# Moving 42 of the weight-scale sums from the attention into the projection, and evicting a finished tile earlier in the DVE's order

## The reference

```
x = x + attn(layernorm(x));  x = x + ffn(layernorm(x))
attn: q, k, v = x@W + x@A@B (16 query heads, 4 key/value heads of 128, rank 16)
      rms norm and rotation of q and k, causal softmax attention -> y
      y minus its part along v;  out = y@Wproj + y@p_A@p_B
ffn:  every weight matrix W (8192 x 2048) becomes clip(round(W/s), -1, 1) * s, s = mean(|W|) + 1e-8
      down(silu(up(x)) * gate(x))
```

## Time and profile before

| | |
|---|---|
| median of three executions | 3892.86 us (3891.25 to 4554.52) |
| the profiled execution's own time | 3895.69 us |
| its span, slowest core | 3894.1 us (cores 3872.2 to 3894.1) |
| granted TensorE clock, mean of a core | 0.977 to 0.983 |
| PE busy, DVE, ACT, GpSimd | 95%, 46%, 24%, 18% |
| front, until the first low-rank product | 0 to 918.6 us |
| projection, four blocks | 918.6 to 1212.3 us |
| feed-forward | 1212.3 to 3894.1 us |

### The profile page before, as it was taken

One profiled execution on the slowest core, in us unless ns is written; L12 is line 12 of the kernel. 1 busy time (PEld: TensorE's weight loads), 2 busy tenths in 40 slices (PEclk: granted clock), 3 DMA queues, 4 the chain that ended last, 5 costly groups with the idle time before them and its releaser, 6 DMA issues.

```text
span 3894.1 us, 52465 instructions; the slowest of 8 cores (3872.2 to 3894.1 us)
## 1 busy us (share of the span) xinstructions
PE 3694.9 (95%) x19512; PEld 1787.0 (46%) x19512; DVE 1773.2 (46%) x2309; ACT 930.3 (24%) x1662; POOL 687.7 (18%) x835
## 2 busy tenths in 40 slices
PE   6898898958998999999999999999999999999999
PEld 4555555534333444444444444444444444444444
DVE  5666676644346333344433334433333443333443
ACT  4566676754111544200000100000100000101000
POOL 3355555445534000000000000000000000000000
PEclk9999999979999999999999999999999999999999
DMA  6577777696334877546422225632222663222364
GB/s 170 159 217 207 204 218 202 200 206 216 126 116 143 302 276 256 191 177 230 173 76 76 76 76 206 227 141 76 76 76 76 230 230 114 78 76 79 110 229 155
DMA packets 123949, 629.65 MB, mean 162 GB/s; under 512 B 13120, under 2 KB 13440, under 8 KB 73008
## 3 DMA queue, kind: packets, MB, share of 16 engines
q1 hardware_dynamic: 96960, 469.80, 35.6%
q0 software_dynamic: 26736, 156.45, 13.1%
HBM read 555.55 MB, written 92.27 MB: 166 GB/s over the span
## 4 chain that ended last, share of the span: by engine, by line
PE 82%; DMA 7%; DVE 5%; issue 3%; POOL 2%; ACT 1%; DVEq 0%; SPq 0%; POOLq 0%; ACTq 0%
PE accps L1366 67%; PE gps L396 5%; PE accps L1170 4%; DMA pw<-W_gate 3%; PE yps L797 2%; PE sps L769 1%; DMA pw<-W_up 1%; DMA yst<-xb 1%; DMA bm0t<-v_B 1%; DVE pacc L202 1%; DVE slabB L1249 1%; POOL xreg L1208 1%; PE gps L401 1%; DVE ss L436 1%; DMA bm1t<-v_B 0%
## 5 line engine op out<-in xcount | busy, mean ns | idle before, releaser
L1366 PE MATMUL accps<-slabB,xreg 128*128 128x512 bf16 x8192 | 1773.5, 380 | 4.4 <-DVE slabB L1249 4.4
L1366 PEld LDWEIGHTS accps<-slabB,xreg 128*128 128x128 bf16 x8192 | 802.4, 98 | 975.0 <-issue 11.7
L1366 PE MATMUL accps<-slabA,xreg 128*128 128x512 bf16 x4096 | 884.7, 380 | 0.0
L1379 ACT ACTIVATE xreg<-accps,scl 128x512 f32<-128x512 f32 x256 | 175.1, 687 | 2052.4 <-PE accps L1366 2052.4
L1366 PEld LDWEIGHTS accps<-slabA,xreg 128*128 128x128 bf16 x4096 | 400.7, 98 | 483.3
L1334 DVE TENSOR_SCALAR xreg<-xreg,scl 128x2048 bf16<-128x2048 f32 x192 | 247.3, 1288 | 601.9 <-PE accps L1366 577.6
L1337 DVE SCALAR_TENSOR_TENSOR xreg<-xreg,scl 128x2048 bf16<-128x2048 f32 x192 | 453.1, 2360 | 20.4 <-DVE xreg L1334 0.5
L396 PE MATMUL gps<-wq,slabA 128*128 128x512 bf16 (+1 forms) x2048 | 416.9, 335 | 14.8 <-DMA wq<-Wqkv 12.0
L1393 DVE SCALAR_TENSOR_TENSOR xreg<-accps,scl,xreg 128x512 f32<-128x512 f32 x256 | 192.0, 750 | 471.3 <-PE accps L1366 471.3
L1383 DVE TENSOR_TENSOR slabA<-xreg,accps 128x512 bf16<-128x512 f32 x256 | 175.2, 686 | 503.6 <-PE accps L1366 500.4
L781 ACT ACTIVATE pring<-sps 128x512 bf16<-128x512 f32 x510 | 297.7, 610 | 148.6 <-PE sps L769 116.7
(11 more groups left out here) (165 smaller groups left out, 2165.9 us busy)
## 6 DMA issues: line engine op xcount, KB each, us to landing
xreg<-W_down SPq DMA_DIRECT2D x128, 1024.0 KB, 7.8
pw<-W_up SPq DMA_DIRECT2D x128, 512.0 KB, 5.7
pw<-W_gate SPq DMA_DIRECT2D x128, 512.0 KB, 5.7
xreg<-W_up SPq DMA_DIRECT2D x64, 1024.0 KB, 5.1
xreg<-W_gate SPq DMA_DIRECT2D x64, 1024.0 KB, 5.0
xreg<-acc_scr POOLq DMA_DIRECT2D x64, 1024.0 KB, 7.5
acc_scr<-xreg POOLq DMA_DIRECT2D x48, 1024.0 KB, 5.2
outT<-xreg POOLq DMA_DIRECT2D x16, 1024.0 KB, 5.2
```

Source lines behind the costliest of these rows:

```text
L1366: pan_tok[k][tc] = op("tensor", lambda e, tc=tc, dt=dt, mov=mov: e.matmul(bank(st_ + tc), tern[s][:, dt * 128:(dt + 1) * 128], mov, start= ...
L1379: evict[k][tc] = op("scalar", lambda e, tc=tc, cs=cs: e.activation(silu[:, cs], bank(st_ + tc), AF.Silu, scale=scl[:, 1:2]))
```

## The change

It makes two changes to the program:

- The front makes 214 of the 256 sums instead of all: `ABS_A` is 174 instead of 222, and the last group goes from 174 to 214 (`ABS_F`). The other 42 are made in blocks 0, 1 and 2 of the projection, 14 each, all on ACT, with four buffers that lie in the half of `xreg` which holds y of the next block. The loads start behind `proj_post` of tile 0, two sums follow behind each of the tiles 2 to 8, and `load_y(s + 1)` is issued at tile 10, behind a wait for the last sums. In blocks 1 and 2 the calls for tiles 0 to 5 come together, behind `proj_post(s, 5)`. `finish_scale` for both matrices moves from tile 8 of block 0 to tile 14 of block 2.
- In a slot of the attention the functions in `ends` (`y_start` of a tile that ended) are called ahead of ACT's and DVE's queued steps and of the sums, instead of behind them.

```diff
--- before.py
+++ after.py
@@ -141,7 +141,7 @@
                     "pe", "dv", "ac", "po", "gp", "gd", "cst", "cs2",
                         "wc0", "wc1", "wc2", "wc3", "wc4", "wc5", "wc6", "wc7",
                         "wc8", "wc9", "wc10", "wc11", "wc12", "bm0", "bm1",
-                        "xs0", "xs1", "pw0", "pw1", "pw2", "gns", "ys0", "ys1",
+                        "xs0", "xs1", "pw0", "pw1", "pw2", "gns", "pw3", "ys0", "ys1",
                         "wp0", "wp1", "wp2", "wp3", "pab", "ld0", "ld1", "ld2",
                         "yl0", "yl1", "xl0", "xl1", "xl2", "xl3", "xl4",
                         "xo0", "xo1", "xo2", "xo3", "xo4",
@@ -176,14 +176,14 @@
             pieces = [(mi, src[k][:, h * 1024:(h + 1) * 1024], mi * 128 - 64 + 2 * k + h)
                       for mi, src in ((1, w_up), (2, w_gate))
                       for k in range(64) for h in range(2)]
-            piece_next = [0]
+            piece_next, piece_end = [0], [0]
 
             pend = []
 
             def abs_load(s, slots, sems, frees):
 
                 n = piece_next[0]
-                if n >= len(pieces):
+                if n >= piece_end[0]:
                     return
                 piece_next[0] += 1
                 mi, src, col = pieces[n]
@@ -610,6 +610,8 @@
             ev_tok = {}
             pw_free = [None, None, None]
             pw_args = (pw, ("pw0", "pw1", "pw2"), pw_free)
+            ABS_A, ABS_F = 174, 214
+            piece_end[0] = ABS_F
             ABS_0 = NT - 3
             def unit_finish(j):
                 t = TO[j]
@@ -670,7 +672,6 @@
             NPAIR = len(pairs)
             PER = NPAIR // HKV
             LAG = 3
-            ABS_A = 222
             W_LATE = 8
 
             def yts0():
@@ -1021,11 +1022,15 @@
                             ends.append(weigh(n_av, n))
                             n_av += 1
 
+                    for fn in ends:
+                        if fn:
+                            fn()
+
                     lag = 0
                     if n < NPAIR and not (r < 10 and g < HKV - 1):
 
                         lag = (ABS_0 + n * (ABS_A - ABS_0) // (3 * PER) if g < HKV - 1 else
-                               ABS_A + (r + 1) * (256 - ABS_A) // PER) - n_abs
+                               ABS_A + (r + 1) * (ABS_F - ABS_A) // PER) - n_abs
                     if not due(for_act, n) and lag > 1:
                         abs_sum("scalar", *pw_args)
                         n_abs += 1
@@ -1036,9 +1041,6 @@
                     if n > 8 and lag > 0 and (not busy or lag > 3):
                         abs_sum("vector", *pw_args)
                         n_abs += 1
-                    for fn in ends:
-                        if fn:
-                            fn()
                     if n == PER * (HKV - 1) + 2:
                         wait("gpsimd", gemm_end[HKV - 1])
                         for i in range(16):
@@ -1052,7 +1054,7 @@
                                         y_dram[0].rearrange("p i t -> p (i t)"))
                 while pend:
                     abs_sum("vector", *pw_args)
-                assert not for_act and not for_pool and piece_next[0] == 256
+                assert not for_act and not for_pool and piece_next[0] == ABS_F
 
 
                 while next_slot:
@@ -1149,7 +1151,7 @@
                     .rearrange("(i p) t -> p i t", p=128))
 
             def lowrank_y(s):
-                wait("tensor", pab, yl_tok[s], ya_bank_free[0], front_bank[0])
+                wait("tensor", pab, yl_tok[s], *ya_bank_free, front_bank[0])
                 for k in range(ND):
                     tp = op("tensor", lambda e, k=k: e.matmul(
                         bank(0)[0:48, :], pa[:, k, :], yts[s % 2][:, k, :],
@@ -1422,11 +1424,34 @@
                 acc_free[s] = [a]
 
             load_x(0, 0)
-            load_y(1)
+
+
+
+            def piece_args(s):
+                return ([xf(16 * ((s + 1) % 2) + 4 * i, 1024) for i in range(4)],
+                        ("pw0", "pw1", "pw2", "pw3"), piece_free)
+
+            piece_free = [None] * 4
+
+            def block_pieces(s, i):
+                args = piece_args(s)
+                if i == 0:
+                    piece_end[0] = ABS_F + 14 * (s + 1)
+                    piece_free[:] = [blk_end[s - 1]] * 4 if s else [None] * 4
+                    if s == 0:
+                        wait("sync", *front_early)
+                    for k in range(4):
+                        abs_load(k, *args)
+                for _ in range(2):
+                    if i >= 2 and pend:
+                        abs_sum("scalar", *args)
+                if i == 10:
+                    assert not pend
+                    wait("sync", *piece_free)
+                    load_y(s + 1)
+
             early = []
             for s in range(NB):
-                if 1 <= s < NB - 1:
-                    load_y(s + 1)
                 lowrank_y(s)
                 if s == 0:
                     left = 1
@@ -1442,6 +1467,7 @@
                     load_x(1, 0)
                     for i in range(5):
                         proj_post(s, i)
+                        block_pieces(s, i)
                 else:
                     for i in range(3):
                         proj_mm(s, i)
@@ -1465,10 +1491,15 @@
                         load_x(s + 1, 0)
                     proj_post(s, 4)
                     proj_post(s, 5)
+                    if s < NB - 1:
+                        for i in range(6):
+                            block_pieces(s, i)
                 for i in range(5 if s == 0 else 6, ND):
                     proj_mm(s, i)
                     proj_post(s, i)
-                    if s == 0 and i == 8:
+                    if s < NB - 1:
+                        block_pieces(s, i)
+                    if s == NB - 2 and i == 14:
                         up_s = finish_scale(1, 64, 128, bank(0))
                         gate_s = finish_scale(2, 192, 128, bank(0))
                         ya_bank_free.append(gate_s)
```

## The result

The changed kernel is slower, by under 1%: it takes 1.0076 times as long as the kernel before (95% interval 1.0054 to 1.0099), some 30 us. Two of its five executions, and one of the four of before, had a lower granted clock on a whole die, and such executions are left out of the ratios and times given here. The profiled execution took 3921.13 us (span 3919.6), that of before 3895.69 us (3894.1): +25.4 us, where the prediction had -3.6.

The account below looks back on a forecast made before the run. Feed-forward matmuls, untouched, take two thirds of the span; the three-buffer ring paces the attention, PE the projection. Terms -51 - 5 + 12 + 40.4 = -3.6 us on 3895.69 us (median 3892.86): forecast 3889 us, 8-in-10 range 3838 to 3930.

Parts of the forecast that it names:

- (a): Groups 0 to 2 of the attention: 48 fewer sums cut most waits for pieces, gain 51 us (15 to 68).
- PE's own pace: Attention, groups 0 to 2: 1.25 us a slot (one score matmul), from the best 40 us, against 1.45 in steady windows.
- (b): Attention slots: evicting a finished tile ahead of DVE's queued step gains 5 us (loss of 5 to gain of 15).
- the ring: Attention: three buffers reused for pieces (half weight panels whose absolute values are summed), allowing one per 2.4 us.
- The slot near 1.3 us: Sign for groups 0 to 2: steady windows in the profile after would show slots near 1.3 us.
- The waits for pieces: Sign for groups 0 to 2: DVE's waits for pieces would fall from 98 us to about a quarter.
- (c): Last group of the attention: 34 planned sums become 40, at 2.4 us each less some cover, loss 12 us (0 to 17).
- (d): Projection: 14 sums in each of blocks 0 to 2 delay y's load and ACT's squares; losses 2.4, 14.8, 23.2, together 40.4 us.
- T14: Projection: end of a block's last of 14 sums, at 1.7 us a piece; 75.5 us into block 2.
- The half clock: Projection: after an idle stretch PE runs at 1.2 GHz, costing 2.65 us each time.
- Rival C: Slower: projection pieces at 2.5 us each, loss there 72, sum +28, 3921 us; decides from 1.8 us a piece; chance 0.21.
- Rival D: Attention slot stays at 1.45 us, waits passing to GpSimd's and ACT's chains; +47, 3940 us; chance 0.10.

## Why the prediction failed, step by step

**(a), the step that failed.** "The best 40 us have PE busy throughout ... I take that as PE's own pace. So the loss against PE's pace is 330 x 0.20 = 66 us." Both ends of the 0.20 were wrong. PE's pace is 1.29 us, as the run without sums shows in two windows of 130 us, with PE busy 98% of them. And the 1.45 us came from windows that held passages between groups; 1.40 is the slot away from them, so the excess there was 0.11 us. In the passages 48 fewer sums hardly helped: 60 slots in 100 us became 63, and without any sums there are 73. That these slots are lost to the sums made up behind the ten slots without one is my reading, and no run shows it. The ceiling was 52 us, not 66. The share that I took was about right: -41.2 of 51.8 is 0.80 and in the mean 32.7 of 44.6 is 0.73, and the -56 for (a) and (b) together was 0.85 of 66. One step on the way did not follow either: the prediction says that the ring can't serve PE's own pace, but by its own figures the ring gives a piece per 2.4 us and the plan asks for one per 2.44, so it could just serve it. The slot near 1.3 us that I named as the sign to look for did come, with 1.29, which shows that a sign can be met while the sum is not. The gain fell short by 14.8 us on the slowest cores and by 23.3 in the mean. The waits for pieces fell to under a half, not to a quarter.

**(b)** was right in that it is small: a gain of 5 us in one pair, a loss of 2 in the other. DVE's waits for PE doubled, but the order alone did not do it: from 185 us to the last group they were 28.3 us before, 31.5 with the order alone, 39.8 with the moved sums alone and 58.3 with both.

**(c)** was right: +15.2 on the slowest core and +10.1 in the mean for a predicted 12, and six sums back give 11.1.

**(d)** had the mechanisms right and their sizes 10.8 us too small, 51.2 for 40.4. Block 0: the first sum ended 46.1 us into the block (predicted 43.6) and a piece took 2.1 us, not 1.7. Four loads of x of 1 MB had been issued just ahead of the pieces and two stores of 1 MB ran beside them, where block 1 had one of each; that this is why is likely, and no run isolates it. PE stood 14.7 us, not 7.4, for y. Block 1: 1.73 us a piece, but the first sum ended at 57.4 us, not 53.4; the wait was 14.8 us, not 12.1. Block 2: 1.82 us a piece, T14 at 81.0 us, not 75.5; the squares added 10.6 us (predicted 11.7), PE stood 22.0 us (predicted 18.0). The half clock cost 1.4 to 2.0 us each time, not 2.65. The slower pieces make 13 x (0.41 + 0.03 + 0.12) = 7.3 of the 10.8 us; the late first sums add to it, and the cheaper half clock takes some back. What I did not see is that y was the first of three waits, which ended 83, 89 and 96 us behind the start of block 0; it does not change the sum, but a remedy drawn from y alone gained 3.8 us of the 54.

Together: 14.8 + 3.2 + 10.8 us, and 0.4 in block 3, make the 29.2 us between -3.6 and +25.6 (the feed-forward gave 0.1 back). The largest share is (a)'s, so the step that failed is its excess of 0.20 us a slot, which was 0.11. Rival C, the same mechanism at a slower rate, came near with its +28, but that is luck: the pieces took 1.9 us each in the mean, just beyond the 1.8 from which C was to decide and not the 2.5 of its price, and half of what was missing was missing in (a) and (b), which C took over unchanged. Rival D did not happen.

The Trainium skill, page "DMA: Bandwidth & Descriptors", section "Rules for kernel authors", says to issue a DMA early and wait for it late. The runs agree in part: issuing y early took away both waits for it, 14.7 and 14.8 us. But PE then stood 12.8 and 15.8 us at the copy one group of products later, and over three blocks the early load alone gave 3.8 us.

## What to carry to other kernels

Take the pace of an engine from a run without the suspected load, or from several long windows clear of the passages between stages; the best stretch and a window with a passage in it overstate the excess from both sides. When work goes into an in-order queue, list everything behind it and every reader of that, because removing one wait uncovers the next one that ends soon behind it. Here taking three of them away left 33 of the 54 us, and giving the work itself an earlier place in the block, on top of that, left 2. Price each place by what one more piece costs there (1.8 us in the last group, under 1 in the groups before, 0.2 to 0.3 early in a block with 17 or 18), and fill the cheap places first.

## What the runs showed that I had not expected

- With two buffers of 512 KB in use the median landing was 4.6 us, with three 5.6 us: with the third buffer each load took longer, and a piece still came per 2.9 instead of 3.3 us.
- The last group's time is not even in the number of its sums: 16 planned, 108.4 us; 20, 111.6; 34, 137.5; 40, 148.6; and 96.5 with none. The first 20 cost 0.75 us each, those behind 1.8.
- After 14.7 to 22 us without work PE's first group of 16 matmuls took 5.0 to 5.7 us instead of 3.63, in each of the three places, and the granted clock of its first 3 us was 0.50. The length of the gap does not set the price: a gap of 2.23 us in the same trace was followed by a group of 5.30 us, and before the change a gap of 1.12 us, close behind one of 3.11, by the 6.28 us of the earlier trace rows.

```profile
976.00:979.00 3.00, 3.00 (x8) 0.50 1.04 406
...
1009.79 5.30 PE L1172 MATMUL accps<-xreg,slabA 128*128 128x512 bf16 x16 [2.23 <-DVE slabB L1188]
```
